# Mixture of experts behind two attentions on one core: two experts known from the first token, their weights loaded before the routing

## The reference

```python
scores = sigmoid(x @ gate_w.T) + bias          # 16 experts
topk_w, topk_idx = top_k(scores, 4)
topk_w = topk_w / (sum(topk_w) + 1e-20)
cw = sum(one_hot(topk_idx, 16) * topk_w[..., None], axis=1)
g = einsum('th,eih->eti', x, Wg);  u = einsum('th,eih->eti', x, Wu)
zw = silu(g) * u * cw.T[:, :, None]
out = einsum('eti,ehi->th', zw, Wd)
out = out + silu(x @ Sg.T) * (x @ Su.T) @ Sd.T # shared expert
```

## Time and profile before

| | us |
|---|---|
| median of 3 runs | 724.55 (724.33 to 725.87) |
| the profiled execution | 721.26 |
| its span | 719.2 |
| TensorE busy | 681.9 |
| VectorE busy | 341.2 |
| ScalarE busy | 200.6 |
| GpSimd busy | 175.9 |

### The profile page before, as it was taken

The page is one execution under the profiler, slowest core; times in us unless marked ns, Lnnn a source line. Parts: engine busy times, 40 slices in busy tenths (PEclk is TensorE's granted clock), DMA queues, the critical chain, the costliest instruction groups (busy, mean ns, idle before and its releaser), DMA issues.

```text
span 719.2 us, 9656 instructions
## 1 busy us (share of the span) xinstructions
PE 681.9 (95%) x2428; PEld 392.0 (55%) x2429; DVE 341.2 (47%) x831; ACT 200.6 (28%) x562; POOL 175.9 (24%) x226
## 2 busy tenths in 40 slices
PE   5999999999999999999999999999898999999991
PEld 3555344446777777767776665544343444444440
DVE  3898332532223546576675767555132333223330
ACT  4453332323335433333323342231111111111110
POOL 2344310101000000040404324264032322232332
PEclk9999999999999999999999999999999999999997
DMA  9999996004000020010104102028878757866544
GB/s 328 410 420 420 422 422 284 0 6 170 1 0 1 1 88 0 1 59 1 59 1 147 58 1 118 1 88 190 300 180 193 180 102 179 216 140 105 93 61 56
DMA packets 54481, 98.97 MB, mean 138 GB/s; under 512 B 6528, under 2 KB 27776, under 8 KB 53792
## 3 DMA queue, kind: packets, MB, share of 16 engines
q1 hardware_dynamic: 24704, 69.02, 26.0%
q0 software_dynamic: 8816, 18.00, 12.6%
q10 hardware_dynamic: 20928, 11.54, 5.6%
HBM read 44.50 MB, written 54.17 MB: 137 GB/s over the span
## 4 chain that ended last, share of the span: by engine, by line
PE 78%; DMA 10%; DVE 4%; issue 2%; ACT 1%; SPq 1%; ACTq 1%; POOL 1%; POOLq 1%; DVEq 0%
PE ps L1110 44%; PE ps L1271 11%; DMA out<-rq,sidx 8%; PE ps L1240 4%; PE ps L1101 4%; PE ps L1256 4%; PE ps L1189 3%; PE ps L1190 3%; PE ps L1199 2%; DVE rq L910 2%; DMA rq<-in_Wv 1%; PE ps L1209 1%; DMA kv<-in_experts 1%; PE ps L1133 1%; PE ps L1134 1%
## 5 line engine op out<-in xcount | busy, mean ns | idle before, releaser
L1110 PE MATMUL ps<-kv,rq 128*128 x432 | 194.8, 599 | 4.8 <-SPq L482 3.7
L1110 PEld LDWEIGHTS ps<-kv,rq 128*128 128x128 f32 x432 | 79.4, 191 | 93.7 <-issue 93.2
L1110 PE MATMUL ps<-zT,r 128*128 128x256 f32 (+1 forms) x424 | 103.4, 400 | 0.9 <-ACT kv L654 0.9
L1110 PEld LDWEIGHTS ps<-zT,r 128*128 128x128 f32 x424 | 79.5, 190 | 20.2 <-issue 10.2
L582 POOL DMA_INDIRECT out<-rq,sidx x36 | 56.6, 1573 | 116.6 <-DMA out<-rq,sidx 85.2
L1271 PE MATMUL ps<-r 128*128 128x512 f32 x192 | 85.1, 593 | 0.0
L513 POOL TENSOR_SCALAR ve<-mv 128x1 f32<-128x1 f32 x32 | 7.1, 222 | 301.9 <-DVE mv L879 301.9
L692 ACT ACTIVATE r<-ps,snm 128x128 f32<-128x128 f32 x128 | 45.2, 365 | 82.4 <-DVE snm L966 82.4
L1050 DVE TENSOR_TENSOR rq<-ps,rq 128x256 f32<-128x256 f32 x36 | 15.3, 424 | 100.1 <-ACT rq L745 100.1
L1271 PEld LDWEIGHTS ps<-r 128*128 128x128 f32 x192 | 35.2, 190 | 38.3 <-issue 38.3
L745 ACT ACTIVATE rq<-ps 128x256 f32<-128x256 f32 x36 | 13.8, 383 | 128.3 <-PE ps L1110 113.7
(11 more groups left out here) (163 smaller groups left out, 864.4 us busy)
## 6 DMA issues: line engine op xcount, KB each, us to landing
slot_rows<-rq SPq DMA_DIRECT2D x4, 8192.0 KB, 49.0
kv<-in_experts SPq DMA_DIRECT2D x54, 256.0 KB, 5.2
rq<-slot_rows ACTq DMA_DIRECT2D x136, 64.0 KB, 2.8
r<-in_Wq SPq DMA_DIRECT2D x1, 3072.0 KB, 21.1
r<-in_Wo SPq DMA_DIRECT2D x2, 1536.0 KB, 8.3
r<-in_ctx SPq DMA_DIRECT2D x8, 256.0 KB, 8.9
xr<-in_x SPq DMA_DIRECT2D x8, 256.0 KB, 8.7
out<-xr SPq DMA_DIRECT2D x8, 256.0 KB, 2.9
```

Of the source, the lines that this page charges most:

```text
L1110: mm = pe.matmul(out, lhs(k), rhs(k), start=(k == 0), stop=(k == n - 1))
```

## The change

The experts get a new order: first the two best ones of token 0, then the others by number. A new TensorE step `front` (in the list ahead of `way(13, 0)`, so behind the scores of unit 13) multiplies a matrix that repeats the identity's first column with the first two columns of `idxf`; so every partition gets token 0's two best experts. ScalarE copies them out. A new VectorE step `gate_b` (unit 14) makes from them the row `erow`, which takes the place of `iota16` in the comparison, and then does block 0's marking (`assign`), which `gate_v` did before. Block 0's `place` moves from unit 13 to unit 14. SP waits for these two numbers and for the last scores (`s_s`), loads both experts, and then goes on to `head`, `tab` and the row blocks. In `route_loads` the four operations that picked the first two experts are gone.

```diff
--- before.py
+++ after.py
@@ -131,6 +131,9 @@
         ssum = sb("ssum", [P, 4, 4])
         srs = sb("srs", [P, 4, 4])
         gsc = sb("gsc", [P, 4, E])
+        erow = sb("erow", [P, E])
+        front = sb("front", [P, 4])
+        fronti = sb("fronti", [P, 2], I32)
         top8 = sb("top8", [P, 8])
         idx8 = sb("idx8", [P, 8], U32)
         idxf = sb("idxf", [P, 8])
@@ -220,6 +223,8 @@
         s_fill = sem("slot_rows_zeroed")
         s_zs = [sem(f"rows_placed{k}") for k in range(TOPK)]
         s_mk = sem("expert_mask_done")
+        s_top = sem("first_token_sorted")
+        s_front = sem("front_experts_ready")
         s_free = sem("free_column_done")
         s_sl = sem("slots_done")
         s_sc = [sem(f"ids_scattered{k}") for k in range(TOPK)]
@@ -338,7 +343,8 @@
         def way(n, place):
 
             here = [(what, 3, j) if what[:3] == "ln_" else (what, j)
-                    for j in range(J) for off, at, what in WAY[(j >= 4) + (j >= 5)] if at == place and n == 4 * j + off]
+                    for j in range(J) for off, at, what in WAY[(j >= 4) + (j >= 5)]
+                    if at == place and n == 4 * j + off + ((j, what) == (0, "place"))]
             prog.extend(sorted(here, key=lambda step: ("ln_z", "ln_stat").index(step[0]) if step[0] in ("ln_z", "ln_stat") else 2))
 
 
@@ -349,6 +355,8 @@
                 prog.append(("s", n))
             prog += [("gate_v", step[1]) for step in prog[since:] if step[0] == "gate"]
             since = len(prog)
+            if n == 14:
+                prog.append(("gate_b", 0))
             if n < len(lat_units[1]):
                 prog.append(("kv", lat_units[1][n]))
             for j in BESIDE.get(n, ()):
@@ -358,6 +366,8 @@
             q, r = n // 8, n % 8
             if q < 3 and r % 2 == 0:
                 prog.append(("q", q + 1, r // 2))
+            if n == 13:
+                prog.append(("front",))
             way(n, 0)
             if 1 <= n <= NU:
                 prog.append(("t", n - 1))
@@ -377,7 +387,7 @@
         def order(kinds):
             return {step: i for i, step in enumerate(p for p in prog if p[0] in kinds)}
 
-        TRN = order(("a_t", "ln_t", "t", "gate", "place", "count"))
+        TRN = order(("a_t", "ln_t", "t", "gate", "front", "place", "count"))
         KVN = order(("kv",))
         LNN = order(("ln_z",))
         STN = order(("a_stat", "ln_stat"))
@@ -463,12 +473,13 @@
             sp.wait_ge(s_q, 4 * G)
             sp.dma_start(wsh, ws_d).then_inc(s_ws, 16)
 
+            sp.wait_ge(s_front, 1)
+            front_of = [sp.value_load(fronti[0:1, i:i + 1], min_val=0, max_val=E - 1) for i in range(2)]
+            sp.wait_ge(s_s, NU)
+            for i in range(2):
+                load_expert(sp, front_of[i], i * EW, s_wdma[i])
             sp.wait_ge(s_tabl, 1)
-            sp.wait_ge(s_o, NU)
-            first = sp.value_load(head[0:1, 0:1], min_val=0, max_val=E - 1)
-            load_expert(sp, first, 0, s_wdma[0])
             loads = sp.value_load(head[0:1, 2:3], min_val=TOPK, max_val=E)
-            second = sp.value_load(head[0:1, 1:2], min_val=0, max_val=E - 1)
 
             sp.wait_ge(s_tab, 1)
             for k in range(TOPK):
@@ -476,7 +487,6 @@
             for i in range(2):
                 block_of = sp.value_load(tab[0:1, i:i + 1], min_val=0, max_val=P)
                 load_block(sp, block_of, i, s_gx[i])
-            load_expert(sp, second, EW, s_wdma[1])
             for i in range(2):
                 sp.wait_ge(s_wdma[i], 16 * PIECES)
                 sp.sem_inc(s_w, 1)
@@ -705,9 +715,12 @@
                     if j:
                         act.wait_ge(s_mk, j)
                     act.activation(gsc[:, 0, :], ps[:, n % 2, 0:E], ACT.Exp, scale=-1.0).then_inc(s_trc, 1)
-                elif kind in ("place", "count"):
+                elif kind in ("front", "place", "count"):
                     n = TRN[step]
                     act.wait_ge(s_tr, n + 1)
+                    if kind == "front":
+                        act.copy(front[:, 0:2], ps[:, n % 2, 0:2]).then_inc(s_trc, 1)
+                        continue
                     if kind == "count":
                         act.copy(nE, ps[:, n % 2, 0:E]).then_inc(s_trc, 1)
                     else:
@@ -829,9 +842,7 @@
                 link(dve.tensor_scalar(used, nt, 0.0, None, ALU.is_gt))
                 link(dve.tensor_tensor_scan(ordi, one, used, 0.0, ALU.mult, ALU.add))
                 link(dve.tensor_tensor(ordx, ordi, used, ALU.subtract))
-                link(dve.tensor_tensor(ue, used, iota16, ALU.mult))
-                link(chosen(tf[:, 0:1], ordx, ALU.is_equal, 0.0, ue))
-                link(chosen(tf[:, 1:2], ordx, ALU.is_equal, 1.0, ue))
+                link(dve.tensor_tensor(ue, used, erow[:, :], ALU.mult))
                 link(dve.tensor_copy(tf[:, 2:3], ordi[:, E - 1:E]))
                 link(dve.tensor_tensor_scan(endT, one, nt, 0.0, ALU.mult, ALU.add))
 
@@ -840,7 +851,7 @@
                 link(dve.tensor_reduce(tf[:, 5:6], half_tiles, AX_X, ALU.add))
                 link(dve.tensor_scalar(tf[:, 3:4], tf[:, 5:6], 2.0, -5.0, ALU.mult, ALU.add))
                 link(dve.tensor_scalar(tf[:, 4:5], tf[:, 5:6], 2.0, -4.0, ALU.mult, ALU.add))
-                dve.tensor_copy(head[:, 0:5], tf[:, 0:5]).then_inc(s_tabl, 1)
+                dve.tensor_copy(head[:, 2:5], tf[:, 2:5]).then_inc(s_tabl, 1)
 
             def route_columns():
 
@@ -873,6 +884,20 @@
                     dve.wait_ge(s_eg, i - 1)
                 dve.transpose(xT[:, par, :].rearrange("p (k a j) -> p a k j", k=KC, a=4),
                               xrow[:, par, :].rearrange("p (a k i) -> p a k i", a=4, k=KC)).then_inc(s_txc, 1)
+
+            def assign(j):
+
+                link(dve.tensor_tensor(onehot[:, j, :, :],
+                                       idxf[:, 0:TOPK].rearrange("p (k a) -> p k a", a=1).to_broadcast((P, TOPK, E)),
+                                       erow[:, :].rearrange("p (a e) -> p a e", a=1).to_broadcast((P, TOPK, E)),
+                                       ALU.is_equal))
+                link(dve.tensor_reduce(mask[:, j, :], onehot[:, j, :, :].rearrange("p k e -> p e k"), AX_X, ALU.add))
+                dve.tensor_tensor(mcum[:, j + 1, :], mcum[:, j, :], mask[:, j, :], ALU.add).then_inc(s_mk, 1)
+
+                link(dve.tensor_reduce(wsum[:, :], top8[:, 0:TOPK], AX_X, ALU.add))
+                link(dve.tensor_scalar(wsum[:, :], wsum[:, :], 1e-20, None, ALU.add))
+                link(dve.reciprocal(wsum[:, :], wsum[:, :]))
+                link(dve.tensor_scalar(tokw[:, j, :, 1], top8[:, 0:TOPK], wsum[:, 0:1], None, ALU.mult))
 
             def stat(col, src):
                 link(dve.bn_stats(st[:, col % 2, :], src))
@@ -1007,18 +1032,26 @@
 
                     link(dve.max(top8[:, :], gsc[:, 3, :]))
                     link(dve.max_index(idx8[:, :], top8[:, :], gsc[:, 3, :]))
-                    link(dve.tensor_copy(idxf[:, :], idx8[:, :]))
-                    link(dve.tensor_tensor(onehot[:, j, :, :],
-                                           idxf[:, 0:TOPK].rearrange("p (k a) -> p k a", a=1).to_broadcast((P, TOPK, E)),
-                                           iota16.rearrange("p (a e) -> p a e", a=1).to_broadcast((P, TOPK, E)),
-                                           ALU.is_equal))
-                    link(dve.tensor_reduce(mask[:, j, :], onehot[:, j, :, :].rearrange("p k e -> p e k"), AX_X, ALU.add))
-                    dve.tensor_tensor(mcum[:, j + 1, :], mcum[:, j, :], mask[:, j, :], ALU.add).then_inc(s_mk, 1)
-
-                    link(dve.tensor_reduce(wsum[:, :], top8[:, 0:TOPK], AX_X, ALU.add))
-                    link(dve.tensor_scalar(wsum[:, :], wsum[:, :], 1e-20, None, ALU.add))
-                    link(dve.reciprocal(wsum[:, :], wsum[:, :]))
-                    link(dve.tensor_scalar(tokw[:, j, :, 1], top8[:, 0:TOPK], wsum[:, 0:1], None, ALU.mult))
+                    ins = dve.tensor_copy(idxf[:, :], idx8[:, :])
+                    if j:
+                        link(ins)
+                        assign(j)
+                    else:
+                        ins.then_inc(s_top, 1)
+                elif kind == "gate_b":
+                    dve.wait_ge(s_top, 1)
+                    dve.wait_ge(s_trc, TRN[("front",)] + 1)
+                    lo, hi = front[:, 2:3], front[:, 3:4]
+                    link(dve.tensor_copy(fronti[:, :], front[:, 0:2]))
+                    link(dve.tensor_tensor(lo, front[:, 0:1], front[:, 1:2], ALU.min))
+                    link(dve.tensor_tensor(hi, front[:, 0:1], front[:, 1:2], ALU.max))
+                    link(dve.tensor_scalar(gsc[:, 1, :], iota16, -2.0, None, ALU.add))
+                    link(dve.scalar_tensor_tensor(gsc[:, 2, :], gsc[:, 1, :], lo, gsc[:, 1, :], ALU.is_ge, ALU.add))
+                    link(dve.scalar_tensor_tensor(erow[:, :], gsc[:, 2, :], hi, gsc[:, 2, :], ALU.is_ge, ALU.add))
```

(9 more changed lines are left out.)

## The result

| | before | after |
|---|---|---|
| median, runs side by side, us | 723.51 (8 runs, 722.25 to 725.87) | 727.75 (8 runs, 725.63 to 730.24) |
| ratio | | 1.0058, interval 1.0038 to 1.0078 |
| span of the profiled execution | 719.2 | 723.8 |
| its time | 721.26 | 725.63 |

The change made the kernel slower by 0.6%, 4.2 us. I had forecast 4.5 us faster. The profiled spans say the same: 4.6 us more, where the sum said 4.5 less.

The account below looks back on a forecast made before the run. TensorE, busy 95% of the span, was taken to bound the kernel. The terms -5.8 - 1.3 - 1.1 + 3.7 = -4.5 us took 724.55 to 720.0, range 717.4 to 723.2.

Parts of the forecast that it names:

- Taken from the routing: Four VectorE operations, 0.8 us, removed ahead of the table matmuls; TensorE is occupied there without a break, so nothing gained.
- these 3.3 us: Distance of the three runs' median above the profiled execution, added to the profiled forecast 716.8 to give 720.0.
- the early loads: Both first experts loaded behind the last scores: waits before gate_up(0) and gate_up(1) and half clock vanish, 5.8 us gained.
- The new wait for the third block: Possible TensorE wait near gate_up(2) for the third block of rows: taken as 0, with 1.5 us as bound.
- First scatters and order, -2.4 together: In the expert loop: 1.3 us gained at the first four serial scatters, 1.1 us by the new expert order.
- The rival that the new order makes more serial scatters: Two groups of expert openings, five waits instead of three, cost +11.9 in place of -1.1: 733; chance 0.05.
- The new step's stand, +3.7: In the attention TensorE waits at the new step for the sorted index, 3.44 us late plus its passes: 3.7 lost.
- The clock behind it: Rival: the clock falls after the new step's stand in the attention, price 1.8 us, giving 721.8; chance 0.18.
- The range: Measured time expected within 717.4 to 723.2 us, from the bounds of scatters and stand, with the clock and scatter rivals.
- the whole loss at the scatters: The two scatter gains, 1.3 and 1.1 us, fail, leaving only -5.8 + 3.7: 722.4; as a rival, chance 0.14.
- it does not load early: Rival: SP stands at a new wait until the routing, so only the stand is paid: 728.2; chance 0.03.
- VectorE, ScalarE, SP: Added small operations in the attention, ScalarE's two-column copy and SP's reordered queue: no cost, being covered or pushing nothing back.

Follow-up runs that it names:

- e5: The kernel before, unaltered, run for a second trace: 722.38 us, ratio 0.9993.
- e12: e2 with four token-number scatters sent in GpSimd's idle time and the last four held until the load table is copied: 714.19 us, ratio 0.9897.
- e17: The changed kernel as it stands, with e12's two edits at GpSimd: 719.71 us, ratio 0.9972.
- e18: e12 unaltered, run again: 713.85 us, ratio 0.9889.
- e19: e2 with GpSimd waiting, ahead of the last four token-number scatters, until the four before have landed: 714.76 us, ratio 0.9892.
- e1: The changed kernel, unaltered, run again: 730.02 us, ratio 1.0067.
- e2: The changed kernel with the new step put behind the projection work that used to cover the sorted index: 722.45 us, ratio 0.9968.
- e8: The kernel before with its first two experts, as constants, loaded behind the last scores; no new step or order: 724.65 us, ratio 1.0012.
- e13: e9 unaltered, run again on chip 12: 723.49 us, ratio 1.0001.
- e15: e2 with VectorE copying the load table instead of ScalarE: 721.58 us, ratio 0.9969.
- e3: The changed kernel with both expert loads back at their old places, new order and step kept: 725.51 us, ratio 1.0006.
- e4: The changed kernel with only the second expert loaded behind the last scores, the first at its old place: 726.22 us, ratio 1.0001.
- e7: e2 with the table matmuls moved behind the transposes of the shared expert's tiles 4 and 5: 718.01 us, ratio 0.9925.
- e6: e2 with GpSimd sending the last eight token-number scatters only when the load table has been copied: 718.62 us, ratio 0.9918.
- e16: The kernel before with e12's two edits at GpSimd: 725.06 us, ratio 1.0018.
- e9: e2 with eight question-and-answer rounds between VectorE and ScalarE ahead of the table copy: 719.45 us in one run, before 721.76.

## Why the prediction was wrong

**What failed, and where in the text.** The sentence is "Taken from the routing. [...] TensorE is occupied without a break [...] right up to the table matmuls that wait for this chain; nothing." Up to the table matmuls it is right. Behind them the sum has no term at all: it put at nothing the time in which TensorE's signals reach ScalarE. There 8.5 us went in after: the hand-over of the table from TensorE to ScalarE, which took 0.6 us in the trace I read (491.00 to 491.63) and 5.5 in the changed kernel (496.04 to 501.51), with the transposes' copy later still and 1.8 us or so of half clock behind it.

**The sign of it was on the page.** The last line of the sum reads "the median of the three runs lies 3.3 above the profiled one, so 724.55 becomes 720.0". I carried these 3.3 us along as if they were a constant. All three runs (724.33 to 725.87) lie above the profiled execution (721.26), outside a spread of 1.5. Such a distance says that the trace may lack something that the timed runs have. e5's trace shows a candidate: the halt, 4.44 us at the table, in a span longer by 3.8. So the kernel before can pay this already, and what I took to be its ordinary course at 491 to 500 is only one of two. Its medians beside the groups point the same way: 725.42, 723.85 and 723.54 on chips 14, 5 and 12, where signals come late, and 721.76 and 721.27 on chip 15. The spread of the times alone would not tell it: on chip 15, where no trace has the halt, they run from 717.75 to 725.35.

**Why the early loads won nothing then.** In the kernel before the halt and the waits for the weights overlap: while TensorE stands at the table the second expert's load comes in. In e5 the stretch from gate_up(0) to gate_up(3) takes 16.73 us, so against it the early loads' 14.62 win 2.1 us, not 5.8. The 5.8 us were there to win only where no halt is: from the tables to gate_up(3) it is 29.40 us in the first trace of before and 24.34 to 24.83 in e12, e17, e18 and e19. With one it is 32.03 before (e5) and 32.5 to 33.7 with the early loads (after, e1, e2, e8, e13, e15), however exact the 14.62 behind it. And in the traces the halt is longer when no weights are on their way: 7.4 to 8.1 us in all of after, e1, e2 and e8, and 2.4 and 4.4 with the loads at their old place (e3 beside e1 and e2 on chip 14, e5 beside e8 on chip 5; one trace each). e3 shows a reason, GpSimd's pause, but that the pause ends the halt is argued from the coincidence of two rows (500.61 and 501.11) and from e5's; e19, made to show it, ran on the chip on which nothing was late. It remains a guess.

**Point by point.**
- *Early loads, -5.8.* The working is right to the digit for the trace that it was taken from: 19.83 and the 0.57 of idle ahead of it, 20.40 together, became 14.62, in one piece at full clock. What failed is that this trace was taken for every execution; against e5 the same term is 2.1. The new wait for the third block, set at 0, did not come in after, where its transfer had the halt's time as well; without a halt there is 0.38 us of idle ahead of gate_up(2) in e17 and 0.85 in e19, and up to 0.89 (e12) ahead of gate_up(0), for which the sum has no term either.
- *First scatters and order, -2.4 together.* The size was too small: -3.5 (176.61 to 173.11). The first four start 9.12, 5.94 and 6.09 us apart, 21.15 in all (GpSimd's timeline below), where I had set 21.8 and the earlier trace rows has 23.13; no idle of TensorE over 0.6 us is left behind gate_up(0) in after. The size rests on one pair of traces. Over all of them this stretch takes 174.8 to 178.5 us in the old order (five traces) and 172.2 to 175.0 in the new (fifteen). The rival that the new order makes more serial scatters is out: e3, with the order but not the loads, has 174.77.

```profile
530.86 1.65 POOL L592 DMA_INDIRECT out<-rq,sidx  x1 [0.89 <-POOL sidx L585]
...
539.98 1.62 POOL L592 DMA_INDIRECT out<-rq,sidx  x1 [7.27 <-DMA out<-rq,sidx]
...
545.92 1.57 POOL L592 DMA_INDIRECT out<-rq,sidx  x1 [4.11 <-DMA out<-rq,sidx]
...
552.01 1.57 POOL L592 DMA_INDIRECT out<-rq,sidx  x1 [4.32 <-DMA out<-rq,sidx]
```

- *The new step's stand, +3.7.* Right, 3.8. *The clock behind it,* held at 0.18: it came in all five traces that have the stand (after, e1, e3, e4, e17), for 1.5 us (6.83 us for twelve matmuls) to 3.1 (8.40 in e17). It is the second step that failed, the one that took this stand for "a shade under" the one in the earlier trace rows and so for harmless.
- *The range.* With the clock and the whole loss at the scatters the prediction's own terms give 720.0 + 1.8 + 2.4 = 724.2, and its upper end stops at 723.2. The measured 727.75 is above both. It lies next to the 728.2 of the rival "it does not load early" by chance, since the loads were early.
- *VectorE, ScalarE, SP.* Nothing, as forecast.
- *With its terms as measured and without the halt*, the change is worth -5.8 - 3.5 + 3.8 + 1.5 = -4.0. e17 is the nearest run to that: 0.9972, 1.6 us less by the medians, with 3.1 us lost to the half clock in its trace in place of 1.5, and e12's edits at GpSimd in it. So the terms that the sum has were read rightly, but for the half clock; the term that it lacks, 8.5 us in after, is larger than their sum.

**What is shown and what is open.** Shown: the lost time lies between TensorE's signals and the engines that wait for them (after, e1, e2, e7, e8, e15). The waiting engines and their own signals are on time in its first half (e13), and VectorE is no better off than ScalarE (e7, e15). With no scatter of token numbers under way at the table nothing is late there (e6 on chip 5, e16 on chip 12, both chips on which it is late otherwise), and when four of them are moved ahead, the lateness moves with them (e16). The same kernel has it on chip 12 and not on chip 15 (e13, e9), and over all of them: late signals in ten of the eleven traces from chips 14, 5 and 12, the exception being e6; in none of the seven from chip 15.
The scatters are not enough by themselves: the transposes' signal passed at 490.60 in e7, and in e6 scatters run from 491.24 on and nothing is late.

Open is what holds a signal. One thing goes with it that I can't take apart from it: the traces of these executions are incomplete. In the first trace of before and the seven from chip 15 there are 7427 to 7451 recorded increments of semaphores, in after and the eleven from chips 14, 5 and 12 only 6481 to 6581, in e6 too. Up to 300 us all twenty have 1301 to 1305. What is missing begins where GpSimd's scatters begin, is mostly the landings of transfers, and lies thickest around the table: from 480 to 500 us e5 has 111 increments where the first trace of before has 481. Of the 1024 landings of its scatters of rows and token numbers, 478 to 585 are recorded in these twelve and 1021 to 1024 in the other eight. So the recording itself runs short in the same executions, and beside the same scatters. It is not enough for a halt, since e6 has none.
The Trainium skill (page "NOTIFIC — the notification-queue block", section "7.1 Overflow: three behaviours, one of which stalls the engine") tells that the block through which such records leave the chip can drop them or hold up their producer. If that is what happens, the halt belongs to an execution that is recorded, and would not be there in one that isn't. All times here come with records of span and clock, so no run here shows an unrecorded execution.
The Trainium skill (page "Perfetto Trace Analysis", section "Tensor Engine Instruction (MATMUL, LD_WEIGHTS)") tells that the end of a matmul in a trace is computed, and that its signal goes out only when its writes to PSUM are acknowledged. So it can't be told from the rows whether TensorE gave its signals late or they travelled long.

**A version that beats both.** e2's place for the step, with e12's or e19's edit at GpSimd, took 0.989 to 0.990 of before's time on chip 15 (e12, e18, e19). On the chips with the halt e2 took 0.9968, and the fastest were e6 (0.9918) and e7 (0.9925); e12 and e19 were not measured there, and by e16 e12's edit may only move the halt. e18 and e17 differ by the place of the step alone and lie 5.9 us apart, most of the 7.4 by which e18 lies under before.

## What to carry to other kernels

If the profiled execution lies outside the spread of the timed runs, take a second trace before anything is summed up: here a second one, e5, has 4.4 us of wait in the very place that the change makes bare. A wait that is taken away is worth its length only if no other wait stands in the same stretch, so look for the hand-overs between engines that today are hidden under it. And a new step on the engine that sets the time goes behind the work that covers its input, not ahead of it: one line, 5.9 us.

## What the runs showed of the hardware

- ScalarE and VectorE waited 1.8 to 8.1 us for signals of TensorE beside small indirect scatters of GpSimd, in after and on three of four numbered chips (two waits more, of 0.4 and 1.1 us, followed such a one), with the DMA nearly idle beside them (share 0.00 to 0.03 in after) or not (0.6 to 0.9 in e5). The sign is "remote" as a releaser in a program of one core.
- Behind the same stand of 3.18 us the same twelve matmuls took 6.83 us in after, 7.55 in e1, 7.97 in e3, 7.54 in e4 and 8.40 in e17, where 5.32 is full clock: what one fall of the clock costs varied by a factor of two. TensorE's timelines of e1 and e17:

```profile
310.21 7.55 PE L1304 MATMUL ps<-r 128*128 128x512 f32 x12
...
307.61 8.40 PE L1304 MATMUL ps<-r 128*128 128x512 f32 x12
```

- The clock also falls near 157 us in nine of the twenty traces, both with and without the change, behind two idle times of 0.7 us that the first trace of before has as well, at full clock. TensorE's timeline of e12, then the busy times with the clock:

```profile
153.60 1.13 PE L1232 MATMUL ps<-rq,r 96*128 96x512 f32 x2 [0.76 <-DVE rq L967]
155.40 5.59 PE L1242 MATMUL ps<-r,rq 128*128 128x512 f32 x8 [0.67 <-ACT rq L687]
```

```profile
158.00:159.00 1.00, 1.00 (x3) 0.54 (x2) 0.05 (x1) 0.00 (x0) 0.00 (x0) 0.50 0.00 0
```
